# Cross attention on one core: a third head in the first unit, the second half of the first shift issued one unit later on ACT, two transposes of the second batch in exchanged banks

## The reference

```python
Q = (query @ Wq.T + bq).reshape(B, Sq, N_HEADS, D_K).transpose(0, 2, 1, 3)
K = (key_value @ Wk.T + bk).reshape(B, Skv, N_HEADS, D_K).transpose(0, 2, 1, 3)
V = (key_value @ Wv.T + bv).reshape(B, Skv, N_HEADS, D_K).transpose(0, 2, 1, 3)
scores = jnp.einsum('bhqd,bhkd->bhqk', Q, K) / np.sqrt(D_K)
attn = jax.nn.softmax(scores, axis=-1)
context = jnp.einsum('bhqk,bhkd->bhqd', attn, V)
context = context.transpose(0, 2, 1, 3).reshape(B, Sq, D_MODEL)
x = context @ W_o.T + b_o + query
mu = jnp.mean(x, axis=-1, keepdims=True)
var = jnp.mean(jnp.square(x - mu), axis=-1, keepdims=True)
return (x - mu) / jnp.sqrt(var + LN_EPS) * ln_gamma + ln_beta
```

## Time and profile before

| | us |
|---|---|
| median of 3 runs | 141.38 |
| lowest, highest | 141.04, 141.88 |
| the profiled execution | 141.58 |
| its span, first to last instruction | 139.7 |
| PE busy in the span | 130.6 (93%) |
| DVE, ACT, POOL busy | 96.5, 89.8, 82.0 |
| unit (0, 0) on PE | starts at 24.35 |
| unit (1, 0) on PE | starts at 40.94 |

### The profile page before, as it was taken

The page is one execution under the profiler, slowest core; times in us unless marked ns, Lnnn a source line. Parts: engine busy times, 40 slices in busy tenths (PEclk is TensorE's granted clock), DMA queues, the critical chain, the costliest instruction groups (busy, mean ns, idle before and its releaser), DMA issues.

```text
span 139.7 us, 3936 instructions
## 1 busy us (share of the span) xinstructions
PE 130.6 (93%) x1477; PEld 114.9 (82%) x1477; DVE 96.5 (69%) x225; ACT 89.8 (64%) x187; POOL 82.0 (59%) x105
## 2 busy tenths in 40 slices
PE   4999999899989999998999999999999999999960
PEld 4899968689779979797999998999899878878620
DVE  5977799988837874667568856975687787521442
ACT  0778643469485848767775959475957758788620
POOL 8347899995722852205279866740589007498271
PEclk9999999999999999999999999999999999999996
DMA  4996685894379832661235336603270100011102
GB/s 120 325 361 227 224 253 192 270 328 133 90 183 305 253 111 70 218 180 56 66 141 194 110 98 194 237 3 75 90 273 0 41 3 5 9 35 33 38 0 66
DMA packets 16099, 19.59 MB, mean 140 GB/s; under 512 B 2624, under 2 KB 15488, under 8 KB 16080
## 3 DMA queue, kind: packets, MB, share of 16 engines
q1 hardware_dynamic: 14960, 17.42, 38.8%
q0 software_dynamic: 640, 1.64, 4.6%
q10 hardware_dynamic: 480, 0.28, 0.7%
HBM read 6.30 MB, written 0.92 MB: 52 GB/s over the span
## 4 chain that ended last, share of the span: by engine, by line
PE 84%; DVE 9%; DMA 2%; issue 1%; ACTq 1%; POOLq 0%; SPq 0%; ACT 0%; DVEq 0%
PE m_bank L882 20%; PE pv_bank L994 14%; PE mx_bank L943 14%; PE st_bank L976 14%; DVE mx L749 5%; PE m_bank L1026 4%; PE st_bank L882 3%; PE mx_bank L1066 3%; PE m_bank L1005 2%; PE m_bank L903 2%; PE mx_bank L976 2%; DMA q_stack<-shift 2%; PE m_bank L1013 1%; DVE k_hl L722 1%; ACTq L275 1%
## 5 line engine op out<-in xcount | busy, mean ns | idle before, releaser
L749 DVE TENSOR_REDUCE mx<-mx_bank 112x1 f32<-112x375 f32 x128 | 63.7, 540 | 21.3 <-PE mx_bank L943 21.0
L632 ACT ACTIVATE pw<-st_bank 125x448 f32<-125x448 f32 x86 | 45.3, 545 | 17.7 <-PE st_bank L976 17.3
L943 PE MATMUL mx_bank<-k_stack,q_stack 128*112 128x376 f32 x128 | 43.6, 353 | 0.7 <-DVE mx L749 0.4
L976 PE MATMUL st_bank<-q_stack,k_stack 128*125 128x224 f32 x172 | 34.9, 284 | 0.6 <-DMA q_stack<-shift 0.4
L976 PEld LDWEIGHTS st_bank<-q_stack,k_stack 128*125 128x125 f32 x172 | 28.6, 186 | 4.0 <-issue 1.5
L943 PEld LDWEIGHTS mx_bank<-k_stack,q_stack 128*112 128x112 f32 x128 | 22.2, 177 | 3.9 <-DVE mx L749 1.9
L430 POOL TENSOR_TENSOR k_hl<-k_full,k_hl 128x376 fp32r<-128x376 f32 x10 | 10.0, 1002 | 20.1 <-ACT k_hl L549 20.1
L994 PE MATMUL pv_bank<-pw,v_sb 125*17 125x112 f32 x744 | 21.5, 260 | 0.0
L994 PEld LDWEIGHTS pv_bank<-pw,v_sb 125*17 125x17 f32 x744 | 16.7, 97 | 3.1 <-issue 1.8
L882 PE MATMUL m_bank<-w_hl,c_hl 128*125 128x256 f32 x126 | 18.2, 282 | 0.0
L882 PEld LDWEIGHTS m_bank<-w_hl,c_hl 128*125 128x125 f32 x126 | 17.2, 186 | 0.0
(11 more groups left out here) (113 smaller groups left out, 179.2 us busy)
## 6 DMA issues: line engine op xcount, KB each, us to landing
k_stack<-k_hl SPq DMA_DIRECT2D x48, 188.0 KB, 2.5
c_raw<-ctxT SPq DMA_DIRECT2D x7, 375.0 KB, 3.9
q_stack<-q_hl SPq DMA_DIRECT2D x9, 112.0 KB, 3.1
x_space<-x_nat SPq DMA_DIRECT2D x4, 224.0 KB, 3.0
out<-yo SPq DMA_DIRECT2D x8, 112.0 KB, 2.0
pw<-wT SPq DMA_DIRECT2D x2, 256.0 KB, 5.3
q_stack<-q_hl POOLq DMA_DIRECT2D x3, 168.0 KB, 2.8
q_stack<-q_hl SPq DMA_DIRECT2D x3, 168.0 KB, 2.9
```

The costliest lines, as they stand in the source:

```text
L632: nc.scalar.activation(p_tile[0:KC, n % PR, :, :], st_of(n)[0:KC, 0:4 * Q].rearrange("p (j q) -> p j q", j=4), ACT.Exp, scale=float(DK) ** ...
L749: nc.vector.tensor_reduce(mx[b % 2][:, h % 2, q_pair(h // 2):q_pair(h // 2) + 1], mx_bank[n % MR][0:Q, 0:KV], axis=AX_X, op=ALU.max, negat ...
L943: nc.tensor.matmul(mx_bank[n % MR][0:Q, 0:KVP], q_stack[k][:, side, q_pair(h // 2), b - Q_STACKS[k][0], :], k_stack[b % 3][:, h // 2, :], ...
L976: last = nc.tensor.matmul(st_of(n)[0:KC, k * 2 * Q:(k + 1) * 2 * Q], k_stack[i % 3][:, 2 * g + k, c * KC:(c + 1) * KC], q_stack[qk][:, :, ...
```

## The change

Three edits. In unit (0, 0) three heads of the maximum pass are done instead of two, so every later head has its place one head earlier, and the last unit with heads, (6, 2), has one head instead of two. ACT's wait for the second half of batch 0's shift, with the two DMAs, stands after the exponential of unit (0, 2) instead of that of unit (0, 1). In the bank lists MT(2) and OT(0) change places: MT(2) goes into `m_bank[1]`, OT(0) into `m_bank[0]`.

```diff
-    M0_JOBS.append(("MT", _i + 1))
-    M1_JOBS.append(("OT", _i - 1))
+    (M0_JOBS if _i > 1 else M1_JOBS).append(("MT", _i + 1))
+    (M1_JOBS if _i > 1 else M0_JOBS).append(("OT", _i - 1))
...
-FIRST_HEADS = ((2, 2, 2, 2, 2, 2, 2, 2, 1, 1, 1, 1), (2, 2, 2, 2, 2, 2, 1, 1, 1, 1, 1, 1))
+FIRST_HEADS = ((3, 2, 2, 2, 2, 2, 2, 2, 1, 1, 1, 1), (2, 2, 2, 2, 2, 2, 1, 1, 1, 1, 1, 1))
...
-                    if u == 1 and i == 0:
+                    if u == 2 and i == 0:
                         act.wait_ge(shift_ready, 2)
```

## The result

The changed kernel takes 139.73 us (median, 139.71 to 139.85) beside 141.21 for the kernel before (140.90 to 141.88): a ratio of 0.9905 with a 95% interval of 0.9882 to 0.9928. The ratio makes 1.34 us on 141.21; the two medians themselves lie 1.48 apart. A second measurement gave 0.9892 (0.985 to 0.9934). The forecast was 140.2, 1.2 us less, on a base of 141.38. The profiled execution took 139.73 with a span of 137.8.

What follows compares the result with a forecast made beforehand. PE, busy 93% of the span, was taken as the bound. Terms 0.52 + 0.46 + 0.11 + 0.17 - 0.05 = 1.21 us took the median from 141.38 to 140.2 us, with a range of 139.8 to 141.3.

Steps and rivals of the forecast that it cites:

- Unit (0, 0) to (0, 4): Start of batch 0: DVE's reductions are the bound; PE reaches (0, 4) at the old 29.8 us, one head ahead.
- ACT's pay-back: ACT before (0, 5): +0.46 us for the head and -0.45 for the exponential cancel; 0.05 us booked as loss for rounding.
- (1, 0) and the 0 for MT(1): Units (0, 8) to (1, 0): MT(1)'s wait shrinks, but shift 1's DMA still holds (1, 0) at 40.94; gain 0.
- (1, 8): Unit (1, 8): with the bank swap K(4, 0) no longer waits for DVE's split of shift 2; gain 0.52 us.
- (2, 6) and (3, 6): Transposes in batches 2 and 3: heads 63 and 79 come one place earlier; gains 0.46 and 0.11 us.
- The head: Unit (6, 2), where PE is packed, has one head less; its 177 ns weight load gives a gain of 0.17 us.
- The sign of being wrong: Prediction wrong if (1, 0) starts after 41.2 or before 40.7, or a later (i, 0) has a new wait over 0.2 us.
- (A): Unit (0, 6): the second half lands late, at 32.8 to 33.0, costing 0.3 to 0.47 us: 140.5 to 140.7; chance 0.17.
- (B): Unit (4, 0): gains eaten at shift 4's DMAs if POOL does not move; 0.6 us left in all, 140.8; chance 0.10.
- (C): Unit (0, 0): DVE loses what PE wins; (0, 5) up to 1.2 us later, nothing changes: 141.4; chance 0.10.
- (D): Unit (0, 6) held 2.8 us by the second half landing at 35.3; net +1.6, slower at 143.0; chance 0.07.
- (E): An edit does not do what it says, as at (2, 6): 0.46 to 0.57 us missing, 140.7; chance 0.08.

Runs made afterwards that it cites:

- the repeat: The changed kernel measured once more, nothing altered, against the kernel before: ratio 0.9892 (0.985 to 0.9934).

## Why the prediction was right, step by step

**Unit (0, 0) to (0, 4).** Right: DVE is the bound, PE comes out with one head more at the old time. It is 0.11 late at (0, 4) (4.52 against 4.41 from the anchor), which (0, 5) takes up, as that one waits for ACT.

**ACT's pay-back.** Right, and the two halves of it are now shown apart: +0.61 at (0, 5) for the head, -0.45 for ACT's edit alone, 0.00 for both together (booked: +0.46, -0.45 and 0.05). The head's part alone was undersized by 0.15. The two issues took 1.48 us in that run instead of 1.31, and the exponential of (0, 2) stands right behind them: it starts 4.43 from the anchor instead of 3.81. Why the issues took longer is not shown; with head and ACT's edit they took 1.44, and there (0, 5) did not move.

**(1, 0) and the 0 for MT(1).** Right to 0.03: the wait at MT(1) went, that at (1, 0) grew to 1.16 (forecast 1.2), and the unit did not move. The version with MT(1) in (0, 7) confirms the mechanism: 1.04 us earlier at the split gave 0.93 at (1, 0).

**(1, 8).** Forecast 0.52. From (1, 8) to (1, 9) it takes 26.80 - 25.31 = 1.49 us from the anchor, where it took 27.38 - 25.37 = 2.01: 0.52, and 0.51 for the swap alone.

**(2, 6) and (3, 6).** Forecast 0.46 and 0.11; by the table 0.47 and 0.14, and the stretches are 0.93 and 0.81 where 0.93 and 0.82 were read off batches 3 and 4. **The head**: forecast 0.17; from (6, 0) to the end 0.13. From (6, 2) to (6, 3), past the missing head, the gain grows by 0.23 us, and by (6, 5) 0.09 of it is lost again, in the changed kernel as in the run with the third head alone; what takes it is not shown.

**The range.** The measured time is 0.47 below the forecast. 0.17 of it is the base: the forecast was set on the median of three runs, 141.38, and the comparison has the kernel before at 141.21. 0.13 is the sum, which had 1.21 where the anchor shows 1.34; most of it is the 0.05 booked as lost at (0, 5), where (1, 0) came 0.03 earlier instead. The 0.17 left is inside the scatter of the medians, with 0.03 of it from rounding 140.17 to 140.2. The lower end stood 0.4 below the forecast, so it held any two of the three and not all. The kernel before scatters by 1 us between executions (140.90 to 141.88), the changed one by 0.14 in its first four runs and 0.80 in the next six.

**What it said of the waits.** The search of the weight loads left some out: 0.34 us at (2, 1) for an exponential, and 0.34, 0.47 and 0.43 in the last ten us of the span. None of them moved (0.33, 0.34, 0.48 and 0.42 after), so the sum did not suffer. The sign of being wrong, (1, 0) before 40.7, was given from the span's start, and by that clock it came true: the unit starts at 40.37. From the anchor it is 15.52 against 15.55, which is 40.91 by the clock of the kernel before. The sign should have been set from the anchor.

**The rivals.** (A) did not come true in the changed kernel, and that is luck, for the 0 was taken for a reason that does not hold. The prediction put the second issue at 28.97, behind the context load at 28.86. In that order the half ends with the context load, whose last packet ends at 32.30 in the kernel before; with the 0.67 us to PE that makes 33.0, and (0, 6) would have waited the 0.47 of the rival. In the changed kernel the second issue (28.44) was 0.11 us ahead of the context load (28.55), and in the repeat 0.01, with no wait. Where the load came first, the units waited 0.06, 0.28 and 0.49 us. The step "it is now ahead of the second" was wrong for the measured profile by that 0.1. The term was also in the trace, though not in the rows: the half's last packet ended at 31.31, which with 0.67 us is 0.5 us ahead of the 32.50 at which PE needed it. (B) did not come true: (4, 0) starts at 58.30 from the anchor, as much earlier as (3, 7), so POOL's chain moved with PE. The limit of this kind exists, as the run with one more head shows, but for the keys of batch 6. (C) is excluded by (0, 5), (D) by (0, 6), (E) by the rows of (2, 6).

## What to carry to other kernels

A wait removed ahead of a transfer that something else anchors is not a gain but a longer wait at the transfer; ask what starts the transfer and move that, as MT(1) one unit earlier did for another 0.9 us. An instruction that fills an engine's idle time costs what it adds to the queue of the engine that is full there: the same head was 0.42 us cheaper eight units later. And where a loop has the same place in every batch, the batch in which nothing waits gives the price of the wait to a few hundredths.

## What the runs showed of the hardware that was not expected

Two small copies (3.5 KB each) on ACT's queue ended 0.03 to 0.04 us behind the last packet of the copy that SP had issued last ahead of them, in the twelve executions of thirteen in which it can be read: behind a key copy of 188 KB 1.8 to 3.0 us from the second issue, behind a context load of 375 KB 2.7 to 3.2 us. A second issue 0.01 us ahead of that load ended 1.2 us before it, and one 0.07 us behind it ended with it. So a small copy that must land early is to be issued ahead of the large one on the other queue, and with room to spare, since here the order changed from run to run. And the start of the kernel scatters: the same instruction, behind the same work, started at 24.7 to 25.6 us in thirteen profiled executions, which is more than most parts of this change are worth. Profiles of one execution each are to be compared from an instruction behind the start-up, not from zero.
